# Softmax sums turned by VectorE in blocks, in a one-core gated cross-attention kernel

## The reference

```
q = (layernorm(x) @ Wq + bq).reshape(B, L, 8, 4, 128)
k, v = split(ctx @ Wkv + bkv)
scores = einsum('blkgd,bmkd->bkglm', q, k) / sqrt(128)
attn = softmax(scores, axis=-1)
o = einsum('bkglm,bmkd->blkgd', attn, v).reshape(B, L, 4096)
x = x + tanh(g_xattn) * (o @ Wo + bo)
x = x + tanh(g_ffn) * ffn(layernorm(x))
```

## Time and profile before

| | |
|---|---|
| time, median of 3 runs | 2284.32 us (2282.54 to 2286.50) |
| the profiled execution, first to last instruction | 2281.5 us |
| PE busy | 2239.5 us, 98% |
| DVE busy | 1858.9 us, 81% |
| ACT busy | 1667.9 us, 73% |
| POOL busy | 1626.6 us, 71% |
| DMA | 273.97 MB, mean 120 GB/s |

### The profile page before, as it was taken

One profiled execution on the slowest core, in us unless ns is written; L12 is line 12 of the kernel. 1 busy time (PEld: TensorE's weight loads), 2 busy tenths in 40 slices (PEclk: granted clock), 3 DMA queues, 4 the chain that ended last, 5 costly groups with the idle time before them and its releaser, 6 DMA issues.

```text
span 2281.5 us, 37476 instructions
## 1 busy us (share of the span) xinstructions
PE 2239.5 (98%) x12299; PEld 1931.9 (85%) x12299; DVE 1858.9 (81%) x3263; ACT 1667.9 (73%) x3184; POOL 1626.6 (71%) x1373
## 2 busy tenths in 40 slices
PE   7999999999999999999999999999999999999999
PEld 6888888888888888888888888888888888888875
DVE  5898888888888787887888788787887888788786
ACT  4777777777777777777777777777777777777773
POOL 4887888967668678767757778667757657667672
PEclk9999999999999999999999999999999999999999
DMA  7444353455233343426213343333423213222221
GB/s 259 144 152 138 120 166 120 159 189 179 89 116 111 100 160 95 137 80 215 93 46 137 118 132 113 114 133 112 169 85 104 93 63 101 75 91 92 76 90 37
DMA packets 140031, 273.97 MB, mean 120 GB/s; under 512 B 22048, under 2 KB 57408, under 8 KB 139584
## 3 DMA queue, kind: packets, MB, share of 16 engines
q1 hardware_dynamic: 124864, 257.85, 33.2%
q10 hardware_dynamic: 14976, 13.74, 2.9%
HBM read 202.44 MB, written 66.97 MB: 118 GB/s over the span
## 4 chain that ended last, share of the span: by engine, by line
PE 72%; DVE 14%; issue 5%; POOL 4%; ACT 3%; DMA 1%; ACTq 0%; DVEq 0%; SPq 0%; POOLq 0%
PE psW L456 11%; PE psW L458 11%; PE psW L457 11%; PE psS L456 6%; PE psS L457 6%; PE psS L458 6%; PE psW L686 6%; PE psW L689 5%; PE psW L688 5%; DVE psum_ L1444 4%; DVE mrun L1409 4%; DVE pl L1162 3%; PE psW L513 2%; POOL xs L900 2%; PE psW L521 1%
## 5 line engine op out<-in xcount | busy, mean ns | idle before, releaser
L900 POOL TENSOR_TENSOR xs<-xs,mb 128x512 f32<-128x512 f32 x832 | 1064.9, 1304 | 453.2 <-ACT mb L971 453.0
L1409 DVE TENSOR_TENSOR mrun<-psS,mrun 128x512 f32<-128x512 f32 (+1 forms) x704 | 481.1, 683 | 274.7 <-ACT xs L971 272.1
L971 ACT ACTIVATE xs<-psS 128x512 f32<-128x512 f32 x832 | 496.9, 597 | 220.6 <-PE psS L458 209.4
L1162 DVE TENSOR_TENSOR pl<-psP,ph 128x512 fp32r<-128x512 f32 (+1 forms) x672 | 458.1, 682 | 80.2 <-ACT ph L1104 76.1
L1104 ACT ACTIVATE ph<-xs 128x512 fp32r<-128x512 f32 x832 | 520.0, 625 | 3.1 <-PE psW L689 2.9
L1444 DVE TENSOR_TENSOR psum_<-psP,psum_ 128x512 f32<-128x512 f32 (+1 forms) x672 | 456.5, 679 | 2.0
L1101 ACT ACTIVATE psP<-xs 128x512 f32<-128x512 f32 (+1 forms) x672 | 402.3, 599 | 30.9 <-POOL xs L900 13.7
L456 PE MATMUL psS<-ql,kh 128*128 128x512 f32 x832 | 341.6, 411 | 7.6 <-DVE mrun L1409 6.6
L686 PE MATMUL psW<-ph,vh 128*128 128x512 f32 x832 | 335.1, 403 | 3.9 <-POOL pl L904 1.4
L457 PE MATMUL psS<-qh,kh 128*128 128x512 f32 x832 | 327.4, 394 | 0.0
L458 PE MATMUL psS<-qh,kl 128*128 128x512 f32 x832 | 326.6, 393 | 0.0
(11 more groups left out here) (225 smaller groups left out, 4433.8 us busy)
## 6 DMA issues: line engine op xcount, KB each, us to landing
wqh<-scr_wq SPq DMA_DIRECT2D x96, 256.0 KB, 2.6
wql<-scr_wq SPq DMA_DIRECT2D x96, 256.0 KB, 3.0
woh<-scr_wo SPq DMA_DIRECT2D x47, 512.0 KB, 3.3
wol<-scr_wo SPq DMA_DIRECT2D x47, 512.0 KB, 4.2
rbc<-scr_r ACTq DMA_DIRECT2D x52, 256.0 KB, 3.4
scr_wq<-wqh SPq DMA_DIRECT2D x32, 256.0 KB, 2.3
scr_wq<-wql SPq DMA_DIRECT2D x32, 256.0 KB, 2.9
scr_wo<-woh SPq DMA_DIRECT2D x16, 512.0 KB, 2.6
```

The source lines that it names most:

```text
L900: eng.tensor_tensor(tile, tile, mb[:, U % 2, :], ALU.subtract).then_inc(s_sub)
L971: return eng.activation(hi, src, ACT.Copy)
L1162: return eng.tensor_tensor(lo, src, f32(hi), ALU.subtract)
L1409: eng.tensor_tensor(run, psS[0:rows, s % 2, :], a, ALU.max).then_inc(s_m)
```

## The change

In the 52 units of `sum_by_mem` the sums no longer go through TensorE.

- At the end of slot 4 (`LANE`) VectorE turns `psum_` in blocks of 32 by 32 into `rbc`, reading words 16 apart, and reduces each group of 32 to `sf` (128x16): on each block of 32 lanes stand the sums over those lanes.
- At slot 5 (`FOLD`) ScalarE waits for that and issues three DMAs which bring the lane blocks 1 to 3 onto lanes 0 to 31.
- At the start of slot 7 (`WHOLE`) VectorE adds the four (`ssum`, 32x16) and takes the reciprocal. ScalarE writes it at slot 7 and reads it back at slot 8, each one slot later than before, and the division moves from slot 9 to slot 10.
- The two lanes of the last tile are made by ScalarE as a third exponential ahead of `ph`; VectorE's copy is gone.
- The tables no longer have `s` for these units, and other jobs move: the second half of `o` goes to the unit after (`p1`), `v5` to the last slot of kind 0, `q0` ahead of `b` in kind 3, `v11` ahead of `m` in `TURN` and `LAST_BUT_ONE`. The cuts of the output weights in the first batch follow.

```
     def on_slot(V):
-        return 9 if sum_by_mem(V) else 8 if V < UN - 2 else 10 if V == UN - 2 else 6
+        return ON if sum_by_mem(V) else 8 if V < UN - 2 else 10 if V == UN - 2 else 6
+    LANE = 4
+    FOLD = 5
+    WHOLE = 7
+    WRITE = 7
+    READ = 8
+    ON = 10
...
     AT_MEM = [
...
-        "m,v11 - b,v12 k2 p0 s k3 r,p1 q0 - q1 x0 o0,x1",
-        "m q0 b k0 p1 s k1 - q1 k2 - o0 o1",
+        "m,v11 - b,v12 k2 p0 - k3 r q0 p1 q1 - o0,x0,x1",
+        "m - q0,b k0 p1 - k1 q1 - k2 - - o0",
     ]
-    TURN = "m,v11 p0 b,v12 k2 p1 s k3 r q0 - q1 - o0"
+    TURN = "v11,m p0 b,v12 k2 p1 s k3 r q0 - q1 - o0"
...
+            def fold_sums(n):
+                act.wait_ge(s_ls, sums_by_mem(n))
+                for g in range(1, 4):
+                    eng.dma_start(sf[0:32, g, :], sf[32 * g:32 * g + 32, 0, :]).then_inc(s_sf, 16)
...
-                eng.dma_start(scr_r[i % 2], rinv[:, n % 2, :]).then_inc(s_rw, 16)
+                eng.dma_start(scr_r[i % 2], rinv[0:32, n % 2, :]).then_inc(s_rw, 16)
...
+                    if t == NT - 1:
+                        eng.activation(pl[SPARE:SPARE + TWICE, T % RP, :], xs[0:TWICE, T % RX, :], ACT.Exp).then_inc(s_l2)
                     eng.activation(ph[:, T % RP, :], xs[:, T % RX, :], ACT.Exp).then_inc(s_h)
...
+            def lane_sums(n):
+                if lead(n) == 1:
+                    dve.wait_ge(s_a, a_count[NT * n + NT - 1])
+                else:
+                    dve.wait_ge(s_ap, 2 * (n - NU + 1))
+                eng.transpose(rbc[:, :], psum_[:, n % 2, :].rearrange("l (i c) -> l c i", c=16)).then_inc(s_sp)
+                dve.wait_ge(s_sp, sums_by_mem(n))
+                eng.tensor_reduce(sf[:, 0, :], rbc[:, :].rearrange("p (c j) -> p c j", j=32), X, ALU.add).then_inc(s_ls)
+            def whole_sums(n):
+                dve.wait_ge(s_sf, 48 * sums_by_mem(n))
+                rinv_free(n)
+                settle(eng.tensor_reduce(ssum[0:32, n % 2, :], sf[0:32, :, :].rearrange("p g c -> p c g"), X, ALU.add))
+                eng.reciprocal(rinv[0:32, n % 2, :], ssum[0:32, n % 2, :]).then_inc(s_r)
...
                 if sum_by_mem(V):
+                    if t == WHOLE:
+                        whole_sums(V)
                     divide(V, t - on_slot(V))
...
-                    if tt == NT - 1:
-                        eng.tensor_copy(pl[SPARE:SPARE + TWICE, T % RP, :], f32(ph[0:TWICE, T % RP, :])).then_inc(s_l2)
...
+                if sum_by_mem(V) and t == LANE:
+                    lane_sums(V)
```

More of the change, by code:

```diff
@@ L115, in gated_block @@
                     continue
-                if kind == "r" and sum_by_mem(n):
+                if kind in "rs" and sum_by_mem(n):
                     continue
@@ L507, in proj_q, with turn @@
                 emptied(("q", U, h), s_ql, 2 * U + h + 1)
-            def turn(key, src, done, by, v, every_fourth=False):
+            def turn(key, src, done, by, v):
                 o = take(key)
                 for k in range(4):
-                    cols = src.rearrange("l (p k) -> l k p", k=4)[:, k, :] if every_fourth else src[:, k * 128:(k + 1) * 128]
-                    m = eng.transpose(o[:, k * 128:(k + 1) * 128], cols, ident[:, :])
+                    m = eng.transpose(o[:, k * 128:(k + 1) * 128], src[:, k * 128:(k + 1) * 128], ident[:, :])
                 m.then_inc(done)
@@ L621, in job @@
                         pe.wait_ge(s_ap, 2 * (n - NU + 1))
-                    turn(("s", n, 0), psum_[:, n % 2, :], s_su, s_r, n + 1, sum_by_mem(n))
+                    turn(("s", n, 0), psum_[:, n % 2, :], s_su, s_r, n + 1)
                 elif kind == "b":
@@ L1089, in _ @@
                     if t == 0:
-                        if U >= 2:
-                            act.wait_ge(s_su, U - 1)
+                        if U >= 2 and sum_by_mem(U - 2):
+                            act.wait_ge(s_sp, sums_by_mem(U - 2))
+                        elif U >= 2:
+                            act.wait_ge(s_su, sums_by_pe(U - 2))
                     elif t < lead(U):
@@ L1319, in row_max, with rinv_free @@
                                   X, ALU.max).then_inc(s_nm)
+            def rinv_free(n):
+                if n >= 2 and sum_by_mem(n - 2):
+                    dve.wait_ge(s_rw, 16 * sums_by_mem(n - 2))
+                elif n >= 2:
+                    dve.wait_ge(s_rt, sums_by_pe(n - 2))
+            def lane_sums(n):
[11 more added lines that the diff above has]
+                eng.reciprocal(rinv[0:32, n % 2, :], ssum[0:32, n % 2, :]).then_inc(s_r)
             def after_job(kind, n, part):
@@ L1334, in after_job @@
                 elif kind == "s":
[L1335 to L1340, removed]
+                    dve.wait_ge(s_su, sums_by_pe(n))
+                    rinv_free(n)
+                    settle(eng.tensor_reduce(ssum[:, n % 2, 0:4], bank_of(("s", n, 0)).rearrange("p (j k) -> p j k", j=4),
                                              X, ALU.add))
-                    eng.reciprocal(rinv[:, n % 2, :], ssum[:, n % 2, :]).then_inc(s_r)
+                    eng.reciprocal(rinv[:, n % 2, 0:4], ssum[:, n % 2, 0:4]).then_inc(s_r)
                 elif kind == "yl":
@@ L1386, in divide @@
                                              ALU.add, ALU.subtract).then_inc(s_ol)
-            def goes_first(kind, n, part):
-                return kind == "s" and sum_by_mem(n)
             def goes_later(kind, n, part):
@@ L1428, in _ @@
                 for j in jobs.get(s - 1, []):
-                    if (j[0] not in "ms" or not TN - NT < s <= TN) and not goes_first(*j) and not goes_later(*j):
+                    if (j[0] not in "ms" or not TN - NT < s <= TN) and not goes_later(*j):
                         after_job(*j)
@@ L1452, in _ @@
                         after_job(*j)
+                if sum_by_mem(V) and t == LANE:
+                    lane_sums(V)
                 if TN - NT <= s < TN:
                     for j in jobs[s]:
-                        if j[0] in "ms" and not goes_first(*j) and j[1] != UN - 1:
+                        if j[0] in "ms" and j[1] != UN - 1:
                             after_job(*j)
@@ L1499, in _ @@
             dve.wait_ge(s_r, UN)
-            settle(eng.tensor_scalar(rtg[:, :], rinv[:, (UN - 1) % 2, :], tg[:, 0:1], None, ALU.mult))
+            settle(eng.tensor_scalar(rtg[:, :], rinv[:, (UN - 1) % 2, 0:4], tg[:, 0:1], None, ALU.mult))
             for t in range(2):
```

25 lines of the change are left out of this document (14 added, 11 removed), and 6 rows, old and new, of tables (AT, AT_MEM).

## The result

The changed kernel takes 2328.3 us (median; 2325.6 to 2332.2) where the kernel before takes 2284.4 beside it: ratio 1.0196, 95% interval 1.0184 to 1.0208. It is 44 us slower. The forecast was 2273, so 55 us are to be explained.

What follows compares the result with a forecast made beforehand. TensorE's own work was taken to bound the kernel. The terms -24.4 + 11.2 + 2.6 - 2.0 + 1.2 sum to -11.4 us, from 2284.3 to 2272.9, say 2273 us; forecast range 2266 to 2280, wider range 2258 to 2284.

Steps and rivals of the forecast that it cites:

- The bound: Whole kernel: TensorE is busy 2239.5 of 2281.5 us, so time leaves only where its own work shrinks and nothing else delays it.
- -24.4: TensorE, slot 5: four transposes fewer in each of 52 units, 0.47 us a turn, so 24.4 us less.
- VectorE: End of slot 4: block turn taken as 0.68 us (0.60 to 1.0), about 1.4 with second reduction and wait.
- 0 on the path: VectorE's added work at slot 4 is hidden by its idle time; 0.2 to 0.7 us per unit if that cover is gone.
- ScalarE: Per unit a two-lane exponential (0.53 us), three DMA issues at slot 5 (1.0 together) and a wait for lane sums.
- Cover 0 to 0.3: ScalarE's term, closing after the folds' landing, taken as 2 us, with VectorE asking over 3 us later: 0 to 0.3.
- a dear block turn: slower: Rival, slot 5 on ScalarE: price 17 (x - 0.5) + 11 (x - 1), x the turn's excess over 0.60; chance 0.11, late folds included.
- Slot 12 of kind 3, +11.2: Output projection in 14 units of kind 3: TensorE waits 0.8 us each on `ol`, 11.2 us more.
- GpSimd at slot 6, +2.6: TensorE reaches slot 6's value matmuls sooner and waits for GpSimd: 0.07 x 11 in kind 0, 0.3 x 6 in kind 2.
- The maxima's turn, -2.0 and +1.2: `v11` ahead of `m` fills waits in seven units, -2.0 us; later division delays VectorE's last maximum in six of kind 2, +1.2.
- The signs of being wrong: Block turn over 1.5 us, folds landing later than VectorE asks at slot 7, or TensorE's kind 3 waits staying unchanged.

Runs made afterwards that it cites:

- doubling: The kernel before, with the four transposes of the sums made twice into the same bank in the 52 units: 2297.9 us, 15.0 more.
- `oh` and `ol` orders: Folds on SyncE plus `oh` behind the exponentials in kind 3: 2280.0 us; that plus p0 at slot 1, then `ol` ahead of the addition in kinds 2, 3: 2267.4.

## Why the prediction was wrong, point by point

**The bound.** Right in kind, too wide in extent: TensorE's own work sets the time in kinds 0 to 2 from the second batch on. In kind 3 and in the first batch a turn added cost next to nothing (0.04 and 0.08 a unit), so a turn taken away could not be counted there in full. **-24.4** had the right unit price (0.47 read, 0.48 measured) over too many units: 29 of the 52 pay it, and doubling says 15.0. That a turn taken away is worth what one added costs is argued here, not shown.

**VectorE.** The block turn took 1.08 where I took 0.68 and bounded it at 1.0. The Trainium skill (SBUF — State Buffer, section "Door 1: The DMA port swizzle (why `[64,N]` ≈ `[32,N]`)") says that an access which goes on to another line of 16 bytes pays. The trace agrees: 1.54 times with 64-byte steps against words side by side. "0 on the path" held at either length, as the folds on SyncE with both turns show, as long as nobody waits for the lane sums in front of something urgent.

**ScalarE: this is the step that failed.** "0.33 each, 1.0 together" was read from a write to DRAM; the folds took 0.60 each, 1.81 together. "Cover 0 to 0.3" then charged nothing for issues and wait that stand ahead of the second tile's exponentials. They cost 38 us by two runs (38.7 on SyncE, 38.2 behind the exponentials). I had written the place, the chain and the victims down as the rival "a dear block turn: slower", with 0.11, but its price let only the turn's length grow, and gave kinds 2 and 3 0.5 and kind 0 1.0 of spare time and kind 1 and the first batch no part in it. Put the measured excess in (0.48 of the turn, 0.81 of the issues: x = 1.29) and it says 17 x 0.79 + 11 x 0.29 = 16.6, less than half of what was found. For kinds 0, 2 and 3 the price was near: TensorE lost 4.6 us in kind 0 and 3.3 in kind 3 at slot 7, and 6.0 in kind 2 at slot 8, 13.9 together. What it left out was the first batch, 16.5, which I had not looked at, and kind 1, 11.6: the new table leaves its slot 7 free, and TensorE is early at slot 8.

How much spare time there was, the distances on GpSimd tell. Its subtractions and remainders follow one another 1.26 apart there (2.51 for two operations), so a unit's first two remainders start 2.5 apart, before the change as with the folds on SyncE or behind the exponentials. In the changed kernel the second tile's exponential starts 2.1 (kind 1) to 2.6 us (kind 0) later than 0.49 behind its eviction, and the two remainders are 3.8 to 4.4 apart: only 0.7 to 0.8 of the hold was covered (medians by kind, second batch on). With one fold issue the exponential is 0.8 to 1.3 later, the remainders are 2.5 to 3.1 apart, and TensorE loses no more at slots 7 and 8 than before the change, to 0.2 us in all. In this kernel GpSimd, once it runs without gaps, hands on what goes beyond.

**Slot 12 of kind 3, +11.2.** The mechanism was there, and larger: `oh` and `ol` orders gave back 9.6 and 8.0, 17.6 together, kind 2 included, which I had left at no charge. I saw only the wait on `ol`; half of the loss was the remainder `pl`, behind `oh` on ScalarE.

**GpSimd at slot 6, +2.6.** Kind 2 has 2.6 us in six units where I had 1.8; kind 0 has none where I had 0.8. Kind 3 was charged 0 because of `q0`, and its wait grew from 0.3 to 0.5 us in 11 units, 2.2.

**The maxima's turn, -2.0 and +1.2.** TensorE's waits for VectorE's maxima there fell from 12.4 to 8.5 us; of the two terms nothing more was tried.

**Moved jobs.** p0 in the units that are 14 in their batch: nothing charged, 4.6 us. p1 of kind 2: nothing charged, 5.2 us in the first batch, through the buffer that it frees. The exchange of copy and exponential: nothing charged, nothing found.

**The sum.** 2273 + 38.2 + 6.4 (slot 12) + 4.6 + 5.2 + 2.2 = 2329.6, against 2328.3. That it closes is partly luck: by the doubled turn the gain of the first term was up to 9 us too large, and what made up for it isn't shown. Of the first batch's 16.5 us 5.1 lie at slot 7, 3.6 at slot 9 and 7.0 at slots 11 and 12 (the changed kernel against the folds on SyncE); through which waits the hold reaches slots 9 to 12 stays open.

**The signs of being wrong.** None would have told: the block turn stayed under 1.5, TensorE's waits in kind 3 changed, and in the changed kernel the folds landed late in 4 units alone (3.9 us). A sign for a hold on ScalarE itself, such as the time from the eviction to the exponential, was missing.

## What to carry to other kernels

A DMA issue on ScalarE stood in that engine's order here: with its wait it held the exponentials behind it for over 2 us. So put such an issue behind the urgent work of its slot, or on an engine that only issues DMAs. Before charging nothing for a hold, follow it to the next engine that runs without gaps; what goes beyond the spare time ahead of that engine reaches whoever waits for it. When a term is a price times a count, count only the places where the shortened engine is the one that is waited for.

## What the runs showed of the hardware

The DMA issues, after (count, KB each, median us to landing):

```profile
rbc<-scr_r ACTq DMA_DIRECT2D x52, 256.0 KB, 3.4
sf<-sf ACTq DMA_DIRECT2D x156, 2.0 KB, 2.4
...
scr_r<-rinv ACTq DMA_DIRECT2D x52, 2.0 KB, 1.3
```

- A DMA of 2 KB from 32 lanes to 32 other lanes took 0.60 us to issue on ScalarE and 0.59 on SyncE (medians of 156), where one of 2 KB from lanes to DRAM took 0.33 and one of 256 KB back 0.34. Why wasn't tried. The folds landed 2.4 us after their issue (median), where I had taken 2.
- ScalarE issued DMAs while its last exponentials were still at work (1029.65 beside 1029.49 above), and the first issue began before the last exponential did (1029.10), so behind them the same 1.81 us cost nearly nothing. The Trainium skill (Perfetto Trace Analysis, section "DMA Optimizations") says that where the making of descriptors is the bottleneck, balancing the DMAs over the engines that can issue them (sync, scalar, GpSimd) may help. Whether that is what takes the 0.60 us no run shows; moving the issues to SyncE gave 38.7 us here, and moving them behind two instructions of the same engine gave 38.2.
- VectorE's 32x32 block turn of 128x512 took 0.70 us with words side by side, as much as its other 128x512 operations (0.69), and 1.08 with words 64 bytes apart.
